# Page-buffer clears issued from GpSimd's queue instead of SyncE's, in a two-layer attention and mixture-of-experts kernel whose order is written out by hand

## The reference

```python
x = L0_attn_x                                   # (16, 256, 128) f32
x = _layernorm(x + _L0_attn_ref(x, w_qkv, w_out))         # 16 heads of 8, causal
x = _layernorm(x + _L0_ffn_ref(x, ...))                   # 8 experts, top 2, relu, hidden 256
x = _layernorm(x + _L1_attn_ref(x, ...))                  # 16 heads of 8, not causal, biases
x = _layernorm(x + _L1_ffn_ref(x, ...))                   # 15 experts, top 3, gelu gate, plus a shared expert
```

## Time and profile before

| | |
|---|---|
| median of 3 runs | 905.49 us |
| profiled execution | 905.51 us |
| its span | 903.7 us |
| TensorE (PE) busy | 773.8 us, 86% |
| VectorE (DVE) busy | 652.9 us, 72% |
| ScalarE (ACT) busy | 500.9 us, 55% |
| GpSimd (POOL) busy | 426.0 us, 47% |
| packets of queue q1 (SyncE) | 122.06 MB, 52.0% of the 16 DMA engines' span |
| packets of queue q0 (GpSimd) | 20.99 MB, 8.7% |

### The profile page before, as it was taken

One profiled execution on the slowest core, in us unless ns is written; L12 is line 12 of the kernel. 1 busy time (PEld: TensorE's weight loads), 2 busy tenths in 40 slices (PEclk: granted clock), 3 DMA queues, 4 the chain that ended last, 5 costly groups with the idle time before them and its releaser, 6 DMA issues.

```text
span 903.7 us, 23670 instructions
## 1 busy us (share of the span) xinstructions
PE 773.8 (86%) x7908; PEld 514.9 (57%) x7908; DVE 652.9 (72%) x1916; ACT 500.9 (55%) x971; POOL 426.0 (47%) x654
## 2 busy tenths in 40 slices
PE   3799999887999889998999999989888898999900
PEld 2456556545777555554775655544444587789800
DVE  1768777776666579898668899889884354688845
ACT  2157557444656557577666877776656344444300
POOL 4002341242203665576235673567567501677775
PEclk9999989999999999999999999999999999999955
DMA  5796774788777555637875664525241189996723
GB/s 121 131 260 137 191 208 125 202 200 209 197 185 187 126 119 120 154 87 190 212 202 146 174 139 96 112 51 124 55 120 42 48 249 291 329 290 181 213 64 111
DMA packets 118775, 144.56 MB, mean 160 GB/s; under 512 B 13155, under 2 KB 92673, under 8 KB 118657
## 3 DMA queue, kind: packets, MB, share of 16 engines
q1 hardware_dynamic: 108417, 122.06, 52.0%
q0 software_dynamic: 10240, 20.99, 8.7%
HBM read 89.78 MB, written 54.41 MB: 160 GB/s over the span
## 4 chain that ended last, share of the span: by engine, by line
PE 27%; DVE 11%; DMA 6%; issue 6%; POOL 3%; ACT 3%; SPq 0%; POOLq 0%; DVEq 0%; ACTq 0%
DMA G<-yd,ypos 4%; DVE mp L1586 4%; PE bank_N L1498 3%; PE bank_O L1404 3%; PE bank_FH L1486 3%; ACT P L1218 2%; PE pair_T L1385 2%; POOL xs L1149 2%; PE pair_S L1363 2%; PE pair_T L1486 2%; DVE X L1791 2%; PE bank_O L1486 1%; PE pair_S L1486 1%; PE pair_T L1498 1%; PE bank_M L1475 1%
## 5 line engine op out<-in xcount | busy, mean ns | idle before, releaser
L1586 DVE TENSOR_REDUCE mp<-pair_S 128x4 f32<-128x1024 f32 (+1 forms) x248 | 270.3, 1090 | 73.6 <-PE pair_S L1363 71.9
L1218 ACT ACTIVATE P<-pair_T 128x768 f32<-128x768 f32 (+1 forms) x256 | 234.4, 916 | 97.0 <-PE pair_T L1385 93.4
L1163 POOL DMA_INDIRECT G<-yd,ypos x160 | 154.0, 962 | 109.4 <-DMA yd<-yb 57.1
L1149 POOL DMA_INDIRECT xs<-X,ypos x160 | 159.0, 994 | 80.3 <-issue 44.1
L1404 PE MATMUL bank_O<-P,V 128*18 128x256 f32 (+1 forms) x2048 | 112.0, 360 | 1.4 <-ACT P L1218 1.4
L1385 PE MATMUL pair_T<-QK 51*128 51x256 bf16 (+1 forms) x1024 | 95.8, 262 | 11.0 <-ACT P L1218 8.9
L1363 PE MATMUL pair_S<-QK 48*128 48x256 bf16 (+1 forms) x992 | 92.9, 264 | 7.5 <-DVE mp L1586 5.9
L1108 POOL TENSOR_TENSOR rstd<-mv,half 128x2 f32<-128x2 f32 x48 | 9.5, 198 | 167.4 <-DVE mv L1635 167.2
L1404 PEld LDWEIGHTS bank_O<-P,V 128*18 128x18 f32 x2048 | 54.7, 99 | 43.9 <-issue 13.0
L1791 DVE SCALAR_TENSOR_TENSOR X<-G,wk,X 128x128 f32<-128x128 f32 x160 | 56.2, 352 | 31.6 <-DMA G<-yd,ypos 28.2
L1385 PEld LDWEIGHTS pair_T<-QK 51*128 51x128 bf16 x1024 | 47.0, 96 | 33.5 <-ACT P L1218 24.2
(11 more groups left out here) (178 smaller groups left out, 1432.8 us busy)
## 6 DMA issues: line engine op xcount, KB each, us to landing
QK<-wtab SPq DMA_DIRECT2D x62, 257.0 KB, 3.8
W<-w_in SPq DMA_DIRECT2D x46, 321.0 KB, 3.9
yd<-yb SPq DMA_DIRECT2D x53, 256.0 KB
stk<-parts SPq DMA_DIRECT2D x32, 384.0 KB
QK<-stk SPq DMA_DIRECT2D x64, 192.0 KB
xs<-zeros SPq DMA_DIRECT2D x19, 512.0 KB, 7.4
xp<-xs SPq DMA_DIRECT2D x33, 256.0 KB, 5.2
QK<-stk SPq DMA_DIRECT2D x64, 128.0 KB
```

The costliest lines, as they stand in the source:

```text
L1149: pool.indirect_dma_start(xs[g % 2][0:reach(a) * PAGE], bass.IndirectOffsetOnAxis(ypos[L][:, 2 * b + blk, k:k + 1], 0), X[:, 2 * b + blk, ...
L1163: pool.indirect_dma_start(G[i][:, blk, k, :], None, yd[g][0:reach(q) * PAGE], bass.IndirectOffsetOnAxis(ypos[L][:, 2 * b + blk, k:k + 1], 0))\
L1218: act.activation(P[:, i:i + 2, 0:n], pair["T"][:, :].rearrange("p (h c) -> p h c", h=2)[:, :, 0:n], ACT.Exp, scale=SCALE)\
L1586: dve.tensor_reduce(mp[:, a % 2, 0:n, :, 0, p].rearrange("p a r -> p r a"), S, AX.X, ALU.max, negate=True)\
```

## The change

`clear_xs` moves from SyncE to GpSimd. Its source is no longer one row of 1 KB per partition read four times but a tile of zeros that is four times as wide (4 KB per partition), so each partition's part is one contiguous run on both sides. Clear `k` now also waits for the first pair of transposed scores of batch `k // 2`. The tables `BEGINS` and `WARM` have new numbers. The functions of all other steps are as they were.

```diff
-        add(PRM["clear"][0] + PRM["clear"][1] * k, "SP", 0.5, 3.5, "clear_xs", k, after=[("stack", 2 + k // 2)])
+        add(PRM["clear"][0] + PRM["clear"][1] * k, "POOL", 1.1, 3.5, "clear_xs", k, after=[("scores_T", k // 2, 0)])
...
-    "load_first": (84,),
+    "load_first": (42,),
...
-        zeros = sb("zeros", [D, T])
+        zeros = sb("zeros", [D, FILL * T])
...
-            def clear_xs(k):
-                i, lo, hi = FILL_STEPS[k]
-                if k == 0:
-                    sp.wait_ge(fill_sem.sem, 1)
-                dst = xs[i][lo * PAGE:hi * PAGE].rearrange("(p m) d -> p (m d)", p=D).rearrange("p (m c) -> p m c", c=T)
-                sp.dma_start(dst, zeros[:, :].unsqueeze(1).broadcast_to((D, hi - lo, T))).then_inc(fill_signal(k).sem, DMA)
...
+            def clear_xs(k):
+                i, lo, hi = FILL_STEPS[k]
+                if k == 0:
+                    pool.wait_ge(fill_sem.sem, 1)
+                pool.wait_ge(st_ps.sem, st_ps.at(k // 2, 1))
+                dst = xs[i][lo * PAGE:hi * PAGE].rearrange("(p m) d -> p (m d)", p=D)
+                pool.dma_start(dst, zeros[:, 0:(hi - lo) * T]).then_inc(fill_signal(k).sem, DMA)
```

More of the change, by code:

```diff
@@ L432 @@
[L432 to L436, removed]
[3 rows of a table removed]
@@ L440 @@
[L440 to L444, removed]
[12 rows of a table removed]
@@ L649 @@
-WARM = ((3455, "N", 3), (3602, "M", 3), (3937, "M", 3), (4447, "N", 2), (4576, "M", 3), (4851, "M", 4), (5334, "N", 3), (5486, "M", 3),
[11 rows of a table removed]
+    "load_x": (5763, 8395, 8455, 14303,),
+    "load_later": (6416,),
+    "prepare": (7619,),
+    "bias_rows": (10718,),
+    "bias_add": (10779,),
+    "build_w1": (11373, 11584, 13385, 15073, 17084, 19703, 20091, 22229,),
+    "clear_xs": (4962, 7672, 7792, 8771, 9634, 9754, 10767, 10887, 12005, 13060, 13181, 15486, 16975, 17250, 18178, 18874, 18994, 19259, 20187,
+        20691, 22578, 24957,),
@@ new lines @@
+    "spread_parts": (1456, 2519, 3538, 4538, 5721, 8353, 9291, 10440, 13613, 14949, 16437, 17718, 19661, 21911, 23612, 27414, 29940, 32614, 33596,
[3 rows of a table added]
+    "v_keep": (1414, 1594, 1974, 6853, 8294, 9665, 11136, 13342, 14891, 16569, 17967, 20282, 22027, 26331, 28661, 30681, 32345, 33718, 35742, 38589,
+        39853, 42669, 45054, 48250, 50177, 51381, 53395, 55190, 56885, 58973, 60635, 62319,),
+    "stack": (1878, 3068, 3986, 4960, 6192, 8848, 9721, 11148, 14078, 15485, 16859, 19096, 20770, 22439, 24251, 27862, 30362, 33036, 34018, 35999,
+        39051, 40772, 43994, 45191, 48698, 50348, 51542, 54346, 56336, 57088, 59921, 61143,),
@@ new lines @@
+    "max_T": (4374, 4963, 6606, 8416, 10453, 12053, 13596, 15202, 17733, 18932, 20396, 22208, 23863, 25622, 27463, 31296, 33923, 35828, 37621, 40335,
+        42408, 45326, 47499, 49831, 51785, 54086, 56181, 57718, 59545, 61429, 63622, 65347,),
+    "max_keep": (4417, 5003, 6640, 8570, 10471, 12241, 13640, 15364, 17776, 18975, 20610, 22297, 24160, 25966, 27544, 31329, 33988, 35872, 37731,
+        40379, 42442, 45402, 47549, 49875, 52015, 54225, 56215, 57762, 59608, 61473, 63665, 65385,),
+    "max_rows": (4458, 5823, 6903, 8611, 10512, 12282, 13681, 15405, 18009, 19016, 20690, 22714, 25362, 27568, 30094, 32768, 34243, 36224, 37772,
+        40420, 42708, 45473, 47590, 50080, 52056, 54266, 56256, 57803, 59649, 61514, 63706, 65426,),
@@ new lines @@
+    "route_rank": (8791, 10028, 12237, 12890, 16924, 17141, 18423, 19970, 22508, 28113, 28373, 30386, 33663, 33940, 36448, 38427, 40399, 42776,
+        46276, 49526, 53177, 54058, 55819, 59661, 61786, 62003, 62263, 63110, 64998, 65568, 67207, 68653,),
+    "route_pos_mul": (8933, 10170, 12614, 13032, 17095, 17370, 18719, 20145, 22698, 28296, 28962, 30873, 33805, 34082, 36590, 38569, 40553, 42930,
+        46430, 49680, 54085, 54635, 56460, 59815, 61940, 62273, 63506, 63544, 65209, 65930, 67483, 68819,),
@@ new lines @@
+    "scatter": (9874, 10198, 10325, 10452, 11007, 11134, 11711, 11838, 13300, 13427, 13940, 14067, 14194, 14321, 15605, 17123, 17797, 17924, 18051,
[8 rows of a table added]
+    "x_T": (29328, 31498, 32408, 33770, 37314, 39157, 39949, 44037, 47600, 49215, 50262, 52320, 53457, 55521, 58245, 59961,),
+    "x_T_keep": (29378, 31554, 32468, 33832, 37507, 39212, 40112, 44124, 47666, 49270, 50349, 52375, 53569, 55601, 58311, 60016,),
+    "residual_bias": (29785, 31768, 34709, 35061, 38407, 41432, 43603, 46147, 49718, 50005, 51257, 54673, 55410, 57278, 59444, 60557,),
@@ L663, in lay_out @@
+WARM = ((3378, "N", 3), (3539, "M", 3), (3811, "M", 3), (4375, "N", 2), (4459, "M", 3), (4706, "M", 4), (5398, "M", 2), (5431, "N", 2),
[11 rows of a table added]
 def lay_out(steps):
@@ L1065, in _ @@
             run_plan({"max_rows": max_rows, "load_first": load_first, "load_consts": load_consts, "load_xT": load_xT, "load_x": load_x, "load_later": load_later,
-                      "clear_xs": clear_xs, "build_w1": build_w1, "spread_parts": spread_parts, "stack": stack,
+                      "build_w1": build_w1, "spread_parts": spread_parts, "stack": stack,
                       "table_row": table_row, "w_load": w_load, "x_load": x_load, "page_store": page_store,
```

205 lines of the change are left out of this document (94 added, 111 removed), and 244 rows, old and new, of tables (BEGINS, WARM).

## The result

The changed kernel is slower: 922.86 us (median of four runs, 919.93 to 927.50) against 904.21 us for the kernel before beside it (four runs). The ratio is 1.0209, with a 95% interval of 1.0133 to 1.0286. Forecast were 891 us and a range of 877 to 911; the result lies outside it, on the other side. A second comparison, in the last but one group of experiments, gave 1.0131 (1.0062 to 1.0199). Both intervals lie above 1; whether the loss is more or less than 2% they leave open.

What follows compares the result with a forecast made beforehand. TensorE was taken to set the pace until layer 1's pages, then GpSimd's gathers. From 905.5 us, 14.6 us came off for the clears; other terms were 0, with 0.4 us inside the rounding: 891 us, range 877 to 911.

Steps and rivals of the forecast that it cites:

- What bounds the kernel: Whole kernel: TensorE sets the pace until layer 1's pages are under way, then GpSimd's gathers, 1.27 us apart.
- the third fact: SyncE's queue, 97.67 to 208 us: seven pairs of clears hold it for 44.4 us, some 35 us of it standing still.
- Clears off SyncE's queue, -14.6 us: TensorE, 95 to 235 us: 7.7 us of waits gone, 3.5 us from the clock, 3.4 us of other idle time.
- The sign that I named: SyncE's queue: if the prediction is right, `stack` steps take near 2.2 us everywhere.
- The two terms for the clock and for other idle time: TensorE, 95 to 235 us: half of 7.0 us lost to clock, 3.5 us, and a third of 10.1 us idle, 3.4 us.
- The lower end of the term: TensorE, 95 to 235 us: nothing at all is won if the transfers stay as late as they are.
- Clears on GpSimd, 0: GpSimd's queue: 22 clears at 1.3 us each, covered by GpSimd's waits for VectorE, cost 0; without that cover 13 us.
- The last rival: GpSimd: clears held 3.2 to 4.5 us each delay normalisation and the router's transposition, which TensorE awaits; 917 us, chance 0.12.
- SyncE's order, 0.4 us: Kernel start: q and k weights issued ahead of the second input, one issue less before TensorE's first matmuls, gives 0.4 us.
- The moved places on the other engines, 0 with a bound of 5 us: Engines other than SyncE: many small edits, each under a microsecond, of either sign; 0, bound 5 us to either side.
- this way to be wrong: Whole kernel: layer 0 gains its 15 us and the rearranged order loses it again behind 300 us.
- The first, that only issue time is won: SyncE's queue: transfers stay as late, 9 us of issue time won, a third reaching TensorE, 3 us; 902 us, chance 0.22.

Runs made afterwards that it cites:

- the kernel cut at batch 14: The change's order on every engine up to batch 14's deviations of layer 0, the order of before behind it; 1060.29 us against 1073.59 for the kernel before, 0.9881.

## Why the prediction was wrong

*What bounds the kernel.* The gather stage kept its 120 us, as forecast, and the 11.4 us that the change is behind at layer 0's experts in the table are still there at the end; a gain ahead of 295 us, which was to carry through, never came. Wrong in the third fact. "SyncE's queue is held up by the clears" takes the instruction that stood for the cause of its standing. The rows showed only that pairs of clears took 3.2 us each; that each pair of the earlier trace rows but the last came directly behind a table piece or a residual load was in the order, and I did not ask what the queue would do with the next transfer.

*Clears off SyncE's queue, -14.6 us.* This is the step that failed. I took "all of the 7.7 us of waits for late head layouts and maxima as gone". With the clears alone moved the waits for head layouts and maxima were 3.1 us where the kernel before beside it had 5.0, and those for inputs and pages rose from 2.6 to 8.5 us; the time was 901.99 us against 904.04. The sign that I named, `stack` steps near 2.2 us everywhere, failed with them: the one of batch 9 took 10.10 us. The two terms for the clock and for other idle time hung on the first and fell with it. The lower end of the term, nothing at all, lies in the measured interval (4.7 us less to 2.4 us more); the 14.6 us do not. This holds for the old order around the clears.

*Clears on GpSimd, 0.* Right, and cheaper than priced: 0.59 us instead of 1.3, none longer than 0.76. The last rival, which decides from 2.8 us per clear, falls. Its 917 us is the forecast number nearest to the measured 922.86 and 915.44, but by luck: it came from held clears on GpSimd, and none was held.

*SyncE's order, 0.4 us.* The start was mis-sized: TensorE's first wait shrank by 0.7 us, from 4.22 to 3.53, and the change is 4.5 us ahead at batch 3's deviations in the first pair of profiles and 2.9 in the second. With SyncE's order of before it is 0.7 us behind the kernel before. Past that, the same order puts two table pieces in a row ahead of row maxima and inputs, and TensorE's waits for DMAs between 95 and 235 us are 18.1 us instead of 9.5 with the order of before. In the whole time SyncE's new order still gains, 10.8 us.

*The moved places on the other engines, 0 with a bound of 5 us.* The second step that failed, and the one behind the loss. Between the clears alone and the change with SyncE's order of before only those places differ (the clears' among them): 24.2 us. With SyncE's new order beside them the whole new order costs 915.44 - 901.99 = 13.5 us. I had called them "many small edits, each under a microsecond and of either sign"; one of them puts a combination 3.4 us ahead of its gather's landing and costs TensorE 3.65 us and the clock behind it. The rest of the 13.5 us is placed by the table and not explained. The prediction named this way to be wrong, an order that loses behind 300 us what layer 0 gains, but gave it no price.

*The rivals.* The first, that only issue time is won, gave 902 us; the clears alone took 901.99 us. That the numbers agree so closely is luck, since the measured difference is 2 us with an interval that holds zero. The Trainium skill, DMA: Bandwidth & Descriptors, "Issuing engines are not separate DMA queues", says that moving the issue to another engine saves only the time to start the transfers. The trace agrees: the two queues' shares of the DMA engines are 52.1 and 8.6% before and 47.2 and 12.1% with the clears moved, 60.7 and 59.3% together, and the time is the same. The rival's chance of 0.22 was too small, and none of the rivals held a loss from the order itself.

## What to carry to other kernels

A DMA that takes long to issue is not by that the cause of the hold: ask what was issued ahead of it, in the other queues too, and which transfer will stand there once it is gone. An unurgent transfer behind a burst of small ones can be the cheapest thing to have there: here, in the old order at 904 us, its removal gave nothing back that could be measured. And where a change comes with a new order of hundreds of steps, the order is a term of its own: look in it for consumers that moved closer than a transfer's landing time (here 3.3 us from a gather's issue to the combination behind it) to their gather or load, one by one, before it is costed at zero.

## What the runs showed of the hardware that was not expected

The same programs ran in two kinds of surroundings, 904 and 1071 to 1085 us for the kernel before, and a change that costs 1.3 to 2.1% in the first cost nothing in the second. TensorE's mean granted clock is 0.95 in the first profile of the change and 0.89 in that of the 1075 us kind. The transfers took no longer: SyncE's queue has 47.8% of 918.1 us in the first profile of the change, 439 us, and 41.4% of 1073.9 us in the other, 445 us. What is new are waits that no instruction of the core ends; the profile calls their releaser remote. The largest, with total us, count and longest, in the change run again:

```profile
DVE mp L1587 <- remote: 52.8, 19, 8.0
DVE yb L1774 <- remote: 35.8, 10, 7.2
```

All such waits of that profile sum to 234 us; the profiles of the 904 us kind have none. Those listed are for results of TensorE. The last 96 gathers took 169.6 us there and 119.6 us in the first profile of the change. What causes them stays open; the kernel before was not profiled in such a group. Open too is whether the kernel cut at batch 14, which has the lowest ratio of all, 0.9881, is also faster at 904 us.
